# One core, cross-attention and a routed feed-forward: one maximum over both score banks of a step, top-eight routing, bias sums by DMA, results loaded in pieces

## The reference, cut to what matters

```
def attention(Q, K, V, ..., attn_mask):                  # Q: layernorm(x), K = V = ctx
    q, k, v = (heads of Q @ Wq.T + bq, K @ Wk.T + bk, V @ Wv.T + bv)
    scores = einsum('bhqd,bhkd->bhqk', q, k) / sqrt(8)
    scores = where(attn_mask == 0, -inf, scores)
    out = einsum('bhqk,bhkd->bhqd', softmax(scores), v)
    return out @ Wo.T + bo

def ffn(x, ...):                                         # x: layernorm(x) again
    logits = x @ Wg
    _, topi = top_k(logits, 2)
    gates = softmax(where(one of topi, logits, -inf))
    for e in range(16):
        h = silu(x @ W1[e] + b1[e]) * (x @ W11[e] + b11[e])
        y = y + (h @ W2[e] + b2[e]) * gates[:, e]
    z = silu(x @ Ws1 + bs1) * (x @ Ws11 + bs11) @ Ws2 + bs2
    return y + z

x = x + attention(layernorm(x), ctx, ctx, ...)
x = x + ffn(layernorm(x), ...)
```

## Time and profile before

| | us |
|---|---|
| runs | 316.48 median, 315.83 to 317.02 |
| profiled execution: its own time | 317.54 |
| profiled execution: span, first to last instruction | 315.7 |
| PE busy in the span | 274.9 (87%) |
| DVE busy | 215.1 (68%) |
| ACT busy | 149.6 (47%) |
| POOL busy | 139.0 (44%) |

### The profile page before, as it was taken

The page is one execution under the profiler, slowest core; times in us unless marked ns, Lnnn a source line. Parts: engine busy times, 40 slices in busy tenths (PEclk is TensorE's granted clock), DMA queues, the critical chain, the costliest instruction groups (busy, mean ns, idle before and its releaser), DMA issues.

```text
span 315.7 us, 6054 instructions
## 1 busy us (share of the span) xinstructions
PE 274.9 (87%) x1836; PEld 207.8 (66%) x1836; DVE 215.1 (68%) x713; ACT 149.6 (47%) x313; POOL 139.0 (44%) x227
## 2 busy tenths in 40 slices
PE   7678899988989999998998889999699999999800
PEld 7655455745656556564564467899589999999800
DVE  2856666774786779766797458883257787787806
ACT  3323687644656456564654654422145545545300
POOL 4555433421531234845338402745016576675720
PEclk9797999997999999999999999999999999999975
DMA  6999920000000098000001100118615959685147
GB/s 216 372 369 396 406 102 4 0 0 2 0 1 2 0 354 317 27 27 17 2 0 35 37 1 2 51 34 239 215 41 159 313 163 275 225 267 189 52 139 284
DMA packets 24080, 42.12 MB, mean 133 GB/s; under 512 B 2689, under 2 KB 11777, under 8 KB 24049
## 3 DMA queue, kind: packets, MB, share of 16 engines
q1 hardware_dynamic: 21520, 36.52, 34.4%
q0 software_dynamic: 2528, 5.22, 4.8%
HBM read 27.00 MB, written 14.73 MB: 132 GB/s over the span
## 4 chain that ended last, share of the span: by engine, by line
PE 62%; DVE 20%; DMA 6%; issue 5%; POOL 4%; ACT 2%; POOLq 0%; DVEq 0%; ACTq 0%; SPq 0%
DVE mpad L572 7%; PE ps L1432 6%; PE ps L1438 6%; PE ps L1449 6%; PE ps L1208 5%; PE ps L1166 4%; PE ps L1194 4%; PE ps L1204 4%; PE ps L1167 4%; PE ps L1179 3%; POOL slot_rows L868 3%; PE ps L1192 3%; PE ps L1222 2%; PE ps L1116 2%; PE ps L1117 2%
## 5 line engine op out<-in xcount | busy, mean ns | idle before, releaser
L572 DVE TENSOR_REDUCE mpad<-ps 128x2 f32<-128x308 f32 x128 | 55.3, 472 | 34.1 <-PE ps L1167 33.7
L818 POOL TENSOR_SCALAR ks<-k_stack,cst 128x160 fp32r<-128x160 f32 x64 | 31.2, 501 | 83.0 <-DVE k_stack L557 83.0
L930 POOL DMA_INDIRECT result_rows<-yo,dest x47 | 44.9, 956 | 38.3 <-DVE yo L792 35.3
L995 ACT ACTIVATE pf<-ps 128x512 f32<-128x512 f32 x80 | 46.5, 596 | 16.9 <-PE ps L1208 10.8
L1167 PE MATMUL ps<-ks,qs 96*128 96x308 f32 x128 | 46.0, 416 | 0.0
L1166 PE MATMUL ps<-mq_b,identb 128*128 128x308 bf16 x128 | 38.8, 309 | 6.6 <-DVE mpad L572 6.0
L868 POOL DMA_INDIRECT slot_rows<-xr,slot x32 | 31.5, 985 | 14.4 <-issue 14.0
L1194 PE MATMUL ps<-qs,ks 128*128 128x512 f32 x64 | 37.6, 589 | 0.0
L1166 PEld LDWEIGHTS ps<-mq_b,identb 128*128 128x128 bf16 x128 | 12.5, 98 | 34.4 <-issue 28.9
L1103 ACT ACTIVATE e_s<-ps,wu 128x128 f32<-128x128 f32 x62 | 19.4, 363 | 22.0 <-PE ps L1432 22.0
L1449 PE MATMUL ps<-wd,e_h 128*128 (+1 forms) x188 | 28.7, 277 | 0.6 <-DVE yo L792 0.6
(11 more groups left out here) (190 smaller groups left out, 612.9 us busy)
## 6 DMA issues: line engine op xcount, KB each, us to landing
wu<-w_biased SPq DMA_DIRECT2D x31, 322.0 KB, 4.7
wr<-w_up SPq DMA_DIRECT2D x1, 5152.0 KB, 24.9
w_biased<-wr SPq DMA_DIRECT2D x1, 5152.0 KB, 16.7
slot_rows<-zero SPq DMA_DIRECT2D x1, 3120.0 KB, 27.4
xg<-slot_rows SPq DMA_DIRECT2D x12, 260.0 KB, 3.6
wd<-w_down SPq DMA_DIRECT2D x1, 2048.0 KB, 11.8
xo<-result_rows SPq DMA_DIRECT2D x4, 512.0 KB, 5.4
out<-xs SPq DMA_DIRECT2D x4, 256.0 KB, 2.3
```

The lines of the kernel that those rows point to most:

```text
L572: dve.tensor_reduce(mpad[:, m % 2, q, 96 + 2 * a:98 + 2 * a], ps[:, KS_ + a, 0:2 * SK].rearrange("p (c k) -> p c k", c=2), AX.X, ALU.max, ...
L930: pool.indirect_dma_start(out=result_dram[:, :], out_offset=bass.IndirectOffsetOnAxis(ap=dest[:, n:n + 1], axis=0), in_=yo[:, n % 4, :], i ...
L995: act.activation(pf[:, n % RP, :], ps[:, ST_ + n % 2, :], ACT.Exp, scale=DK ** -0.5).then_inc(exp_done, 1)
```

## The change

- **One maximum for each step.** `row_max` takes both banks in one instruction (four maxima from 2 x 2 x 156 columns; 64 instructions for 128). `score_rows` counts one `smax_mm` after both banks, waits once for the maximum of the step before, ahead of bank 0, and `turn_max` for four instead of eight.
- **The floor column.** Mask and scores get two columns more for each head (156 for 154), whose mask is half the masking constant, so that a query without keys ends with a sum of zero and NaN; `empty_rows` goes.
- **Top-eight.** `pick` takes the eight largest logits of a tile of tokens by one instruction and their places by another (four and four for a batch), turns the two first places into one-hot rows and goes on as before.
- **Shift.** The count of full tiles is an integer shift on 16 columns, three instructions for two over 256 columns.
- **Accumulating DMAs.** `add_bias` and `add_biases` leave DVE; POOL issues two DMAs that add `bo` to `xs` and `bs2` to `wr` in memory, the first in batch 0 at `g = 3`, the second in batch 1 at `g = 1`. The first `add_attention` waits for the one, SP's copy of the weights for the other.
- **Early result loads.** SP loads the first three pieces once 40 tiles are back, the last four tiles as two pieces of two (256 KB each) once all 47 are.

```
-                for a in range(2):
-                    reach(dve, smax_mm, b, 32, 8 * m + 2 * q + a + 1)
-                    dve.tensor_reduce(mpad[:, m % 2, q, 96 + 2 * a:98 + 2 * a],
-                                      ps[:, KS_ + a, 0:2 * SK].rearrange("p (c k) -> p c k", c=2),
-                                      AX.X, ALU.max, negate=True).then_inc(max_done, 1)
+                reach(dve, smax_mm, b, 16, 4 * m + q + 1)
+                dve.tensor_reduce(mpad[:, m % 2, q, 96:96 + HG].rearrange("p (a c) -> p a c", a=2),
+                                  ps[:, KS_:KS_ + 2, 0:2 * SKM].rearrange("p a (c k) -> p a c k", c=2),
+                                  AX.X, ALU.max, negate=True).then_inc(max_done, 1)
...
+                reach(pe, max_done, b, 16, 4 * m + q)
                 for a in range(2):
-                    reach(pe, max_done, b, 32, 8 * m + 2 * q + a - 1)
-                    o = ps[:, KS_ + a, 0:2 * SK].rearrange("p (c k) -> p c k", c=2)
+                    o = ps[:, KS_ + a, 0:2 * SKM].rearrange("p (c k) -> p c k", c=2)
...
                 if step == 0:
                     dve.wait_ge(lg_done, b + 1)
-                    largest(b, lg, m1, one1)
+                    for i, t in enumerate(tiles):
+                        last = dve.max(top[:, i, :], lg[:, t, :])
+                    link(last)
                 elif step == 1:
-                    first_of_largest(b, one1)
+                    for i, t in enumerate(tiles):
+                        last = dve.max_index(place[:, i, :], top[:, i, :], lg[:, t, :])
+                    link(last)
+                    link(dve.tensor_copy(choice[:, :, :], place[:, :, 0:2]))
...
+                    link(dve.tensor_scalar(full_up[:, :], cum[:, b + 1, :], 1.0, float(P - 1), ALU.max, ALU.add))
+                    link(dve.tensor_scalar(full_up[:, :], full_up[:, :], 7, None, ALU.logical_shift_right))
+                    link(dve.tensor_copy(nb[:, b + 1, :], full_up[:, :]))
...
+                    if b == 0 and g == 3:
+                        pool.wait_ge(ld_wr, 32)
+                        pool.wait_ge(xn_done, B)
+                        pool.dma_start(xs[:, :, :], bor[:, :].unsqueeze(1).to_broadcast([P, NT, D]),
+                                       accum_op=ALU.add).then_inc(bo_added, 16)
+                    if b == 1 and g == 1:
+                        pool.wait_ge(ld_b, 16)
+                        pool.wait_ge(ld_d, 32)
+                        pool.dma_start(wr[:, :, WB:WB + D], bsr[:, :].unsqueeze(1).to_broadcast([P, NE, D]),
+                                       accum_op=ALU.add).then_inc(biased, 16)
...
+PIECES = tuple((QT * c, QT) for c in range(B - 1)) + ((NT - QT, QT // 2), (NT - QT // 2, QT // 2))
+            for r in range(4):
+                sp.wait_ge(returned[r], (SETTLED - r + 3) // 4 * 16)
+            for i in range(B - 1):
+                load_results(i)
             for r in range(4):
                 sp.wait_ge(returned[r], (RUN - r + 3) // 4 * 16)
```

More of the change, by code:

```diff
@@ L30 @@
 SKP = 160
+SKM = SK + 2
 NG, HG = 4, 4
@@ L244, in build @@
         ld_u = [sem(f"ld_u{r}") for r in range(RW)]
-        ld_r = [sem(f"ld_r{c}") for c in range(B)]
+        ld_r = [sem(f"ld_r{i}") for i in range(len(PIECES))]
         returned = [sem(f"returned{r}") for r in range(4)]
@@ L420, in pick @@
             def pick(b, step):
-                tiles = slice(QT * b, QT * b + QT)
+                tiles = range(QT * b, QT * b + QT)
+                cols = slice(QT * b, QT * b + QT)
                 if step == 0:
                     dve.wait_ge(lg_done, b + 1)
-                    largest(b, lg, m1, one1)
+                    for i, t in enumerate(tiles):
+                        last = dve.max(top[:, i, :], lg[:, t, :])
+                    link(last)
                 elif step == 1:
-                    first_of_largest(b, one1)
+                    for i, t in enumerate(tiles):
+                        last = dve.max_index(place[:, i, :], top[:, i, :], lg[:, t, :])
+                    link(last)
+                    link(dve.tensor_copy(choice[:, :, :], place[:, :, 0:2]))
                 elif step == 2:
[L429 to L433, removed]
-                else:
-                    dve.tensor_tensor(sel[:, tiles, :], one1[:, tiles, :], one2[:, tiles, :], ALU.add).then_inc(sel_done, 1)
-                    dve.tensor_tensor(four(m2, b), four(m2, b), four(m1, b), ALU.subtract).then_inc(ex_in, 1)
+                    ids = cst[:, C_TILE:C_TILE + NE].unsqueeze(1).to_broadcast([P, QT, NE])
+                    for k, one in enumerate((one1, one2)):
+                        last = dve.tensor_tensor(one[:, cols, :], choice[:, :, k:k + 1].to_broadcast([P, QT, NE]), ids,
+                                                 ALU.is_equal)
+                    link(last)
+                else:
+                    dve.tensor_tensor(sel[:, cols, :], one1[:, cols, :], one2[:, cols, :], ALU.add).then_inc(sel_done, 1)
+                    dve.tensor_tensor(m2[:, cols].unsqueeze(2), top[:, :, 1:2], top[:, :, 0:1], ALU.subtract).then_inc(ex_in, 1)
             def gates(b):
@@ L621, in batch @@
                         block_statistics(1)
-                    if b == 1 and g == 0:
-                        dve.wait_ge(ld_wr, 32)
-                        add_bias(0)
-                        add_bias(1)
                     if g == 3 and b:
@@ L671, in batch @@
                         pick(b - 1, 3)
-                        pick(b - 1, 4)
                     if g or b:
@@ L743, in _ @@
             read_logits(last)
-            for step in range(5):
+            for step in range(4):
                 pick(last, step)
@@ L802, in _ @@
                     meta(n // 4 + 1)
-            for c in range(B):
-                dve.wait_ge(ld_r[c], 16)
-                rows = xs[:, QT * c:QT * c + QT, :]
-                link(dve.tensor_tensor(rows, rows, xo[:, QT * c:QT * c + QT, 0, :], ALU.add))
-                dve.tensor_tensor(rows, rows, xo[:, QT * c:QT * c + QT, 1, :], ALU.add).then_inc(out_done, 1)
+            for i, (t, count) in enumerate(PIECES):
+                dve.wait_ge(ld_r[i], 16)
+                rows = xs[:, t:t + count, :]
+                link(dve.tensor_tensor(rows, rows, xo[:, t:t + count, 0, :], ALU.add))
+                dve.tensor_tensor(rows, rows, xo[:, t:t + count, 1, :], ALU.add).then_inc(out_done, 1)
         @block.gpsimd
```

88 lines of the change are left out of this document (29 added, 59 removed).

## The result

The changed kernel takes 323.77 us (median of 4 runs, 322.47 to 325.05), the kernel before 316.74 beside it; the ratio is 1.0231, with a 95% interval from 1.0176 to 1.0287. In each of the two sessions of e5 to e11 three runs of before lay in a slower state; the medians and ratios are without them. The forecast was 323.5. The profiled execution of the changed kernel has a span of 322.9, 7.2 over the first profile of before.

What follows compares the result with a forecast made beforehand. PE was taken to bound the kernel, with room on DVE. Terms of +12.4, -0.7 and -4.5 gave +7.2 on the profiled 317.54, so 324.7, or 323.5 on the runs' scale; range 315.5 to 333.

Steps and rivals of the forecast that it cites:

- attention: All four batches of head groups: +12.4 us in total, from 4.6 + 0 + 4.3 + 3.5.
- the way to the tiles: From the last turn of the maxima to the first tile: PE's 1.11 wait for the choice shrinks, -0.7 us.
- the tail: After the last scatter: earlier loads and sums and smaller last pieces save 4.5 us (3.7 to 5.8).
- The fused maximum: Attention steps: a 0.80 us maximum makes PE wait, 1.72 from step to step, plain group 5.31 to 6.80.
- hardly waits now: Sign in the changed profile: PE's idle time ahead of the mask's product, small before, reaches 10 us or more.
- Batch 1: Its head groups: +0.6 from waits and -0.6 from removed `add_bias` sums, with a clock fall also going: nothing.
- Top-eight: `pick`: eleven operations of 2.89 us become about 2.0; PE's wait in batch 2 shrinks, -0.7 us.
- Shift, floor column: Tile-count shift and a small memset before the first step: counted at nothing, as they lie beside PE's products.
- Accumulating DMAs: POOL in batches 0 and 1: each holds POOL 0.96 to 15.4 us; low end taken, nothing counted.
- Faster: Rival in attention: PE's other work covers the wait, giving 310 us; decided at a maximum of 0.4; chance 0.11.
- The clock falling again and again: Rival on PE: six to twelve clock falls of about 1.6 us each give 333 to 343 us; chance 0.13.
- POOL held by the DMAs: Rival on POOL: 15.4 us for each DMA makes PE wait, up to 8 more, 331 us; chance 0.08.

Runs made afterwards that it cites:

- e5: Kernel before with only the early result loads and the five pieces at the end: 312.32 us, ratio 0.9896 to the kernel before.
- e11: The changed kernel run once more, unaltered, in a later session: 324.76 us, ratio 1.0305 to the kernel before.
- before again: The kernel before run and profiled once more, unaltered: 313.76 us (a single run), span 312.0.
- e1: Changed kernel with two maxima for each step again and a wait for each bank, all else kept: 308.02 us against 314.14 before, ratio 0.9801.
- e2: Kernel before with only the fused maximum, without the floor column: 330.31 us, ratio 1.0531 to the kernel before.
- e4: Changed kernel with its fused maximum over half of each head's columns (78 of 156), all waits kept: 308.02 us, ratio 0.9795 to the kernel before.
- e6: Kernel before with only the two accumulating DMAs for DVE's sums and the floor column replacing the empty-row test: 312.65 us, ratio 0.9916.
- e9: Changed kernel with two maxima for each step again and eight result row buffers instead of four: 306.98 us against 315.39 before, ratio 0.9739.

## Why the prediction was right

The time was right, 323.5 for 323.77, and so were the side and the main term. The hit to 0.3 is luck: attention came out 1.3 and the way to the tiles 1.4 better than forecast, the tail 2.7 worse, and these cancel. The sum was also counted from a profile of before with two falls of the clock; from before again to the changed profile are 10.9, not 7.2.

*The fused maximum*, right in mechanism and nearly in size: 0.806 for 0.80, a start 0.78 after the step for 0.77, 1.72 from step to step, 6.80 for the plain group. e1, e2 and e4 show that the loss is its own, but for what part of batch 0 the prologue's clock has. By batches +4.9 for +4.6, -0.6 for 0, +3.6 for +4.3, +3.2 for +3.5: 11.1 for 12.4. The four groups of batch 2 took 10.38, 10.91, 10.40 and 11.90 from turn to turn, for 10.5, 11.05, 10.65 and 12.1 in the prediction: what was too large is a little in each, most in the third and fourth, where layer norm and `pick` were taken to stretch a gap of 1.72. Such work fits mostly into gaps that the exchange has made longer. PE's waits ahead of the mask's product grew from 6.0 to 13.7; that it "hardly waits now" was a misreading of before.

*Batch 1* came out near nothing, as forecast, but from larger sides: e2 puts the fusion at +3.1 there, with a fall of the clock in it, e6 the sums at -2.8, against before again; from e1 to the changed kernel, neither of which has the sums or a fall there, it is +3.9. The prediction put 0.6 on the sums and 1.6 on a clock's fall. The first group, without the sums, can fall further than the plain 6.8 that stood in the prediction, as e6's 2.4 shows, where the maxima are two. And the fall of before belonged to that execution, not to the kernel.

*Top-eight*: -0.7 forecast; -2.1 between the two profiles, some -0.9 over all of them. *Shift, floor column*: nothing was forecast, and no row speaks against it. *Accumulating DMAs*: the low end was right enough, 2.4 and 2.1 of POOL's time, covered.

*The tail* was wrong: -4.5 forecast, -1.8 measured from PE's last product to the end. The sums and loads after the last scatter are shorter as worked out (-4.3). The step that failed is the sentence that three pieces load while the last tiles run, at no cost: 1.5 MB of loads ran beside scatters that DVE waits for through the four rows of `yo`. e5 has the same loss without the fusion, and e9 takes it away. What a transfer that is moved earlier runs beside should have been asked, and which buffer waits for that.

The rivals. *Faster* was placed rightly: it was to decide at a maximum of some 0.4, and with e4's 0.48 the step costs next to nothing. The Trainium skill, PSUM — Partial Sum Buffer, Summary: rules for kernel authors, asks to read a bank other than the one PE writes. The traces agree in the full version: one maximum over both banks leaves PE none to write meanwhile, and e2 takes 16 us more. e4 shows that this costs next to nothing where the reading is short enough for PE's other work. *The clock falling again and again* did not come: from 33 us to the end of PE's work the changed kernel's granted clock is at the upper level (2.4 GHz), in both profiles, through 26 of the 30 waits, the longest of 1.5 us among them. One stretch of the changed kernel, batch 1 and what lies around it (columns as above):

```profile
64.00:110.00 46.00, 40.70 (x238) 25.06 (x239) 26.67 (x68) 24.13 (x43) 16.72 (x43) 1.00 0.65 156
```

PE is busy 40.70 of 46.00 there; the 60% of the prediction was worked out for a step alone. Behind the prologue one run with the fused maximum shows a fall, e2, once: from 76 to 78 the clock is 0.50, after 74 to 76, in which PE was busy 0.87 of 2.00 and DVE all the time, with sums of `add_bias` between its maxima. The Trainium skill, TensorE: Matmul & The Clock Gate, A second HAM failure mode: psum-queue depth-cycling, tells of a kernel whose clock swung with such small gaps. The two traces of the changed kernel show no such swing behind 33 us. *POOL held by the DMAs*: 2.4 and 2.1, not 15.

## What to carry to other kernels

When two instructions that free two buffers one after the other are fused into one, the writer loses its overlap: price the exchange from start to start (fill both, read both, pass the semaphore) and compare each gap with the other work the writer has in it, not with the mean gap. A transfer moved earlier isn't free because its own result is in time; look for what is under way beside it and which ring of buffers stands behind that. And before the terms of a sum are taken from one profile, see whether its low-clock stretches are there in a second one.

## What had not been expected of the hardware

- One maximum over two banks (624 columns) took 0.81 us, a pair over 312 each 0.87 from the first's start to the second's end: fusing saves 0.06. Over 312 columns in four pieces of 78 the fused form took 0.48, so the price goes by columns.
- Four top-eights of 16 columns took 0.41 us together and four index searches with their loads 0.67, little more than two ordinary small operations each.
- An accumulating DMA of 1 MB in 2048 rows held POOL 2.37 and 2.12 us and landed after 11.3 and 10.7; it did not hold POOL 16 times as long as the indirect DMA of 128 rows.
- Beside loads of 1.5 MB a scatter of 128 rows came back so late (6.68 us in e1) that DVE stood 2.5 to 4.0 us for it.
- Between 16 us and the end of PE's work, the same kernel ran with two falls of the clock in one profile and none in another, 1.5 us each.
